# The end of the last batch of a two-layer attention kernel: partial products around the last sums, a separate sum buffer for GpSimd, later sums of the third pair

## The reference, cut to what matters

```python
xn = _group_norm(xf, gamma, beta)
qkv = jnp.einsum('oc,bcl->bol', w_qkv, xn) + b_qkv[None, :, None]
...
weight = jnp.einsum('bct,bcs->bts', q * scale, k * scale)
weight = jax.nn.softmax(weight.astype(jnp.float32), axis=-1).astype(q.dtype)
a = jnp.einsum('bts,bcs->bct', weight, v)
hid = a.reshape(b, c, L)
hid = jnp.einsum('oc,bcl->bol', w_proj, hid) + b_proj[None, :, None]
return (xf + hid).reshape(b, c, h, w)
```

## Time and profile before

| | us |
|---|---|
| median of 3 runs (lowest, highest) | 2491.03 (2490.61, 2492.5) |
| the profiled execution, own time | 2492.64 |
| its span in the trace | 2491.1 |
| TensorE busy, share of the span | 2438.5, 98% |
| VectorE, ScalarE, GpSimd busy | 1615.9, 1150.5, 1182.5 |
| stretch of pair 3 of the last batch, from its transpose of the maxima to its last weigh | 2413.9 to 2452.5 |
| stretch from there to the end of the span | 2452.5 to 2491.1 |

### The profile page before, as it was taken

One profiled execution on the slowest core, in us unless ns is written; L12 is line 12 of the kernel. 1 busy time (PEld: TensorE's weight loads), 2 busy tenths in 40 slices (PEclk: granted clock), 3 DMA queues, 4 the chain that ended last, 5 costly groups with the idle time before them and its releaser, 6 DMA issues. The chain is left out here.

```text
span 2491.1 us, 37555 instructions
## 1 busy us (share of the span) xinstructions
PE 2438.5 (98%) x12980; PEld 1615.9 (65%) x12980; DVE 1615.9 (65%) x2161; ACT 1150.5 (46%) x1499; POOL 1182.5 (47%) x590
## 2 busy tenths in 40 slices
PE   8999999999799999999999999999999999999988
PEld 7888888788655566557556655755665575557544
DVE  6455555455667766775777577567857756775776
ACT  3332233223355645654555456355555645553553
POOL 3330000000047665773766667377656755771762
PEclk8999999999899999999999999999999999999999
DMA  6431111013221242215122321512231241213002
GB/s 199 139 111 45 56 67 66 27 42 128 83 95 35 111 144 88 109 32 211 34 97 104 130 101 53 194 43 102 93 144 34 110 175 63 97 31 119 26 26 76
DMA packets 73401, 226.75 MB, mean 91 GB/s; under 512 B 12224, under 2 KB 12224, under 8 KB 72384
## 3 DMA queue, kind: packets, MB, share of 16 engines
q1 hardware_dynamic: 58720, 172.01, 19.6%
q0 software_dynamic: 14560, 52.96, 5.8%
HBM read 141.05 MB, written 71.30 MB: 85 GB/s over the span
## 5 line engine op out<-in xcount | busy, mean ns | idle before, releaser
L591 POOL TENSOR_TENSOR a_all<-a_all 128x1024 f32<-128x1024 f32 x410 | 1010.1, 2464 | 508.2 <-ACT a_all L816 473.3
L816 ACT ACTIVATE a_all<-psum 128x1024 f32<-128x1024 f32 x512 | 496.5, 1022 | 80.3 <-PE psum L1539 67.7
L1104 DVE TENSOR_REDUCE small<-psum 128x2 f32<-128x1024 f32 x326 | 399.6, 1226 | 172.3 <-PE psum L1509 172.1
L1558 PE MATMUL psum<-a_all 128*64 128x512 f32 x2048 | 495.7, 605 | 0.0
L1311 PE MATMUL psum<-r_all 128*128 128x512 f32 x1920 | 454.5, 395 | 6.9 <-DVE r_all L1198 5.8
L1311 PEld LDWEIGHTS psum<-r_all 128*128 128x128 f32 x1920 | 359.4, 189 | 101.6 <-DVE r_all L957 10.2
L1539 PE MATMUL psum<-r_all 64*128 64x512 f32 x3200 | 417.8, 393 | 2.0 <-ACT a_all L816 2.0
L1498 PE MATMUL psum<-r_all 128*128 128x512 f32 x1536 | 364.4, 396 | 5.6 <-DVE r_all L1217 5.6
L1539 PEld LDWEIGHTS psum<-r_all 64*128 64x128 f32 x3200 | 301.7, 186 | 73.2 <-ACT a_all L816 14.0
L1498 PEld LDWEIGHTS psum<-r_all 128*128 128x128 f32 x1536 | 286.0, 189 | 85.9 <-issue 24.4
L1558 PEld LDWEIGHTS psum<-a_all 128*64 128x64 f32 x2048 | 124.0, 136 | 232.5 <-issue 173.4
(11 more groups left out here) (147 smaller groups left out, 2450.9 us busy)
## 6 DMA issues: line engine op xcount, KB each, us to landing
r_all<-w_dram SPq DMA_DIRECT2D x48, 1024.0 KB, 4.9
xn_dram<-a_all POOLq DMA_DIRECT2D x56, 512.0 KB, 7.0
r_all<-xn_dram SPq DMA_DIRECT2D x7, 4096.0 KB, 15.3
a_all<-y_dram SPq DMA_DIRECT2D x9, 2048.0 KB, 10.8
a_all<-x SPq DMA_DIRECT2D x16, 1024.0 KB, 6.5
y_dram<-a_all SPq DMA_DIRECT2D x16, 1024.0 KB, 4.2
out<-a_all SPq DMA_DIRECT2D x32, 512.0 KB, 4.0
a_all<-sums SPq DMA_DIRECT2D x192, 64.0 KB, 2.0
```

Source lines behind the costliest of these rows:

```text
L591: pool.tensor_tensor(p_sum[:, :, cols], probs[:, 0, :, cols] if i == 1 else p_sum[:, :, cols], probs[:, i % SLOTS, :, cols], ALU.add).then ...
L816: act.activation(probs[:, i % SLOTS, :, cols], psum[half][:, :, :], ACT.Exp, scale=SCALE).then_inc(probs_ready, 1)
L1104: dve.reduce_max(max2[:, :, tile, half], psum[3][:, :, :], AX_X).then_inc(work_free, 2)
L1558: last = pe.matmul(psum[2][h * D:(h + 1) * D, half], v_t[:, i, head], probs[:, i % SLOTS, h, half * HALF:(half + 1) * HALF], start=(i == 0 ...
```

## The change

All of it is in the last batch (`last`), most of it in pair 3 (`not more`) and after.

- `sums` of pair 2 moves from the head of pair 3 to behind the scores of i = 2, and goes into psum[3] in place of psum[2]. Its copy on ScalarE stands behind the exponentials of i = 2, its reciprocals on VectorE behind the first and the second `add_last`.
- `end_add` of pair 2 moves from before `max_rows` to behind the two normalises of pair 1. The split of pair 1 on ScalarE moves from before the scores of pair 3 to behind the exponentials of i = 0. Normalise of pair 2 moves from behind `add_last(3)` to behind `add_last(5)`, its high parts to behind the exponentials of i = 7, its low parts to behind the last add.
- GpSimd's adds of pair 3 go into a buffer of their own (`end_sum`, over `y_row`), and no longer wait for the sums of pair 2. `add_last(1)` still does.
- The residual is loaded to `res_end` (over `xn`) during pair 2, and ScalarE scales it from there into `res32` after the last adds, ahead of the high parts of pair 3.
- The projection of half 0 is made in parts, in four banks: j = 0 and 1 of the first tile, then the last sums, j = 0 and 1 of the three others, j = 2 of all four, j = 3 of all four. Half 1 goes tile by tile, the wait for pair 3's split standing ahead of j = 3 of its first tile.
- The output is stored tile by tile, in eight stores of 256 KB.

The diff, cut:

```diff
+        res_end = f(xn[:, 0])
...
+        end_sum = y_row.rearrange("p (h n) -> p h n", h=2)
...
+        def end_bank(t):
+
+            i = t % 6
+            return (psum[3], psum[0], psum[2])[i // 2][:, i % 2]
...
-                if not last:
+                if last:
+
+                    sp.dma_start(res_end, y_v[b]).then_inc(res_loaded, 16)
+                else:
...
-                    sp.wait_ge(pv_done, ONE + (b + 1) * PAIRS * NT)
-                    sp.wait_ge(sum_step, LAST_SUMS + NT - 1)
-                    sp.wait_ge(last_sums, NT - 1)
+
+                    for t, (o, half) in enumerate(proj_tiles(last)):
+                        cols = slice(half * HALF, (half + 1) * HALF)
+                        sp.wait_ge(work_free, proj_used(b, t + 1, last))
+                        sp.dma_start(out_v[b, :, o, cols], res32[:, o, cols]).then_inc(out_stored[o // 2], 16)
...
-                sp.dma_start(res32, y_v[b]).then_inc(res_loaded, 16)
-                for o in range(CT):
-                    sp.wait_ge(work_free, proj_used(b, proj_tiles(last).index((o, NH - 1)) + 1, last))
-                    sp.dma_start(out_v[b, :, o], res32[:, o]).then_inc(out_stored[o // 2], 16)
...
+                    sp.dma_start(res32, y_v[b]).then_inc(res_loaded, 16)
+                    for o in range(CT):
+                        sp.wait_ge(work_free, proj_used(b, proj_tiles(last).index((o, NH - 1)) + 1, last))
+                        sp.dma_start(out_v[b, :, o], res32[:, o]).then_inc(out_stored[o // 2], 16)
...
-                sp.wait_ge(half, ONE + B * CT // 2 * 16)
+                sp.wait_ge(half, ONE + (B + 1) * CT // 2 * 16)
...
-                            if i == 1 and half == 0:
+                            if i == 1 and half == 0 and not last_pair:
...
-                            pool.tensor_tensor(p_sum[:, :, cols], probs[:, 0, :, cols] if i == 1 else p_sum[:, :, cols],
+                            to = end_sum if last_pair else p_sum[:, :, cols]
+                            pool.tensor_tensor(to, probs[:, 0, :, cols] if i == 1 else to,
                                                probs[:, i % SLOTS, :, cols], ALU.add).then_inc(sum_step, 1)
...
+            def scale_res(b, o, res):
+                if o == 0:
+                    act.wait_ge(res_loaded, (b + 1) * 16)
+                act.activation(res32[:, o], res[:, o], ACT.Identity, scale=bn_scale[:, o:o + 1],
+                               bias=res_bias[:, o:o + 1]).then_inc(res_scaled, 1)
...
-                        if p and not more and i == 2:
-                            copy_sums(b, p - 1)
-                        if p >= 2 and i == 2:
+                        if p >= 2 and more and i == 2:
                             for h in range(NH):
...
                         if p and more and i == 0:
-                            copy_sums(b, p - 1)
-                        if p and not more and i in (4, 5):
-                            hid_hi(b, p - 1, i - 4)
+                            copy_sums(b, p - 1, psum[2][:, 0])
+                        if not more:
+                            if i == 0:
+                                for h in range(NH):
+                                    hid_hi(b, p - 2, h)
+                            if i == 2:
+                                copy_sums(b, p - 1, psum[3][:, 0])
+                            if i == NT - 1:
+                                for h in range(NH):
+                                    hid_hi(b, p - 1, h)
...
-                    copy_sums(b, PAIRS - 1)
+                if last:
+
+                    act.wait_ge(sum_step, LAST_SUMS + NT - 1)
+                    act.wait_ge(last_sums, NT - 1)
+                    for o in range(CT):
+                        scale_res(b, o, res_end)
+                else:
+                    copy_sums(b, PAIRS - 1, psum[1][:, :, :])
...
-                act.wait_ge(res_loaded, (b + 1) * 16)
-                for o in range(CT):
-                    act.activation(res32[:, o], res32[:, o], ACT.Identity, scale=bn_scale[:, o:o + 1],
-                                   bias=res_bias[:, o:o + 1]).then_inc(res_scaled, 1)
+                if not last:
+                    for o in range(CT):
+                        scale_res(b, o, res32)
...
+                    if not more:
+                        end_add(pairs - 1)
...
-                        end_add(pairs)
+                        if p < PAIRS - 2 or not last:
+                            end_add(pairs)
                     else:
-                        invert_sums(b, p - 1, 0, CT)
                         for i in range(1, NT):
                             add_last(i, pairs)
-                            if i == CT - 1:
+                            if i in (1, 2):
+                                invert_sums(b, p - 1, (i - 1) * 2, 2)
+                            if i == 5:
                                 for h in range(NH):
                                     normalise(b, p - 1, h)
-                            if i in (5, 6):
-                                hid_lo(b, p - 1, i - 5)
+                        for h in range(NH):
+                            hid_lo(b, p - 1, h)
...
+                    if last:
+                        ps = end_bank(t)
...
-                        pe.wait_ge(sums_copied, ONE + pairs)
+                            pe.wait_ge(sums_copied, ONE + pairs)
...
-                    done = pe.matmul(to, ones64[:, 0:D if wide else QUARTER], p_sum[:, h, half * HALF:(half + 1) * HALF],
-                                     start=True, stop=True)
+                    of = end_sum[:, h] if last and half == 0 else p_sum[:, h, half * HALF:(half + 1) * HALF]
+                    done = pe.matmul(to, ones64[:, 0:D if wide else QUARTER], of, start=True, stop=True)
...
-                    if p and not more:
-
-                        pe.wait_ge(o_ready, ONE + pairs)
-                        sums(pairs - 1, psum[2][:, 0])
...
+                        if not more and i == 2:
+                            sums(pairs - 1, psum[3][:, 0])
                         next_max()
                         if i:
                             weigh(b, p, i - 1, more)
...
+                def proj_steps(to, o, half, js):
+                    cols = slice(half * HALF, (half + 1) * HALF)
+                    slot, piece = o // 2, o % 2
+                    for j in js:
+                        for k, (w, m) in enumerate(THREE):
+                            done = pe.matmul(to, w_s[:, slot, piece, w, j], hid[:, m, j, cols], start=(j == 0 and k == 0),
+                                             stop=(j == CT - 1 and k == 2))
+                    return done
+
+                def hid_made(pairs, half):
+                    pe.wait_ge(hid_lo_done, HID0 + (b * PAIRS + pairs) * NH - (NH - 1 - half))
...
+                tiles = proj_tiles(last)
                 if last:
-                    sums(b * PAIRS + PAIRS - 1, last=True)
+                    for slot in range(2):
+                        pe.wait_ge(ws_loaded[slot], (loads + 3) * 16)
+
+                    pe.wait_ge(sums_copied, ONE + b * PAIRS + PAIRS - 1)
+                    pe.wait_ge(probs_ready, ONE + (b + 1) * PAIRS * 2 * NT)
+                    hid_made(PAIRS - 2, NH - 1)
+                    for t in range(CT):
+                        work.next()
+                        proj_steps(end_bank(t), *tiles[t], range(CT - 2))
+                        if t == 0:
+                            sums(b * PAIRS + PAIRS - 1, last=True)
+                    hid_made(PAIRS - 1, NH - 1)
+                    for t in range(CT):
+                        proj_steps(end_bank(t), *tiles[t], (CT - 2,))
+                    hid_made(PAIRS, 0)
+                    for t in range(CT):
+                        proj_steps(end_bank(t), *tiles[t], (CT - 1,)).then_inc(work_full, 1)
+                    for t in range(CT, 2 * CT):
+                        n, _ = work.next()
+                        if t == CT:
+
+                            pe.wait_ge(o_ready, ONE + (b + 1) * PAIRS)
+                        if t >= 6:
+
+                            pe.wait_ge(work_free, n - 6)
+                        proj_steps(end_bank(t), *tiles[t], range(CT - 1))
+                        if t == CT:
+                            hid_made(PAIRS, 1)
+                        proj_steps(end_bank(t), *tiles[t], (CT - 1,)).then_inc(work_full, 1)
...
-                for t, (o, half) in enumerate(proj_tiles(last)):
-                    cols = slice(half * HALF, (half + 1) * HALF)
-                    slot, piece = o // 2, o % 2
-                    if o == 0:
-
-                        pe.wait_ge(hid_lo_done, HID0 + (b + 1) * PAIRS * NH - (NH - 1 - half))
-                    if half == 0 and piece == 0:
-                        n_load = (loads + 3 + slot) - (1 if last and slot else 0)
-                        pe.wait_ge(ws_loaded[slot], n_load * 16)
```

(35 more changed lines are left out.)

## The result

| | before | after |
|---|---|---|
| median (lowest, highest), us | 2491.77 (2490.61, 2492.75) | 2474.84 (2473.4, 2477.71) |
| ratio to before, 95% interval | | 0.9933 [0.9918, 0.9948] |
| profiled execution: own time, span | 2492.64, 2491.1 | 2477.71, 2476.1 |
| transpose of pair 3's maxima, last batch, start | 2413.94 | 2416.43 |
| from there to the end of the span (the *stretch*) | 77.2 | 59.7 |

The changed kernel is faster by 16.9 us in the medians. The two profiled executions differ by 15.0 only, because the one of after came 2.5 us later to the transpose. Ahead of it only one thing was changed, the residual's load, which SyncE issues at 2384.25. It doesn't explain the 2.5 us: the changed kernel's second profile, with the same load, reached the transpose at 2413.20.

What follows compares the result with a forecast made beforehand. TensorE was taken as the bound, 98% of the span, with two waits in the last batch. Head -5.95, last add +0.6, end -9.7, store -0.4 make -15.4 us: median 2491.03 becomes 2475.6, range 2472 to 2481.

Steps and rivals of the forecast that it cites:

- likeliest case: Whole kernel: all terms come out as summed, median 2475.6 us; chance 0.68.
- The head: Start of pair 3: scores no longer wait for pair 2's last add and sums; -5.95 us.
- the moved sums: Pair 2's sums, now behind the scores of i = 2, take 1.87 us of TensorE with nothing beside them.
- The last add: End of pair 3: VectorE's last add ends 2.85 us behind the last weigh, before 2.23; +0.6 us.
- the order of turns between VectorE and GpSimd: Pair 3's adds alternate; pair 2's two normalises run behind GpSimd's seventh add, which ends at 2445.9 us.
- The exclusion: VectorE's adds, normalises and low parts exclude GpSimd's adds; without any lock the sum would be 1.6 us shorter.
- The end: Last sums to last matmul: partial projection matmuls cover the wait, 20.4 us in place of 30.1; -9.7 us.
- The clock's part: At the end, the low clock over the first projection matmuls costs 2.5 us, part of the 9.7.
- Half 1's split: At the end, split ready at 2462.8 us, TensorE asks for it at 2463.05.
- The residual's move: Residual's load leaves the end, issued at about 2381.8 us, 70 us before use: worth nothing.
- the store: Last output store is half as large; gain between 0 and 0.8 us, taken as 0.4.
- The rival that the clock falls in a hole that is left: TensorE's remaining idle at head or last sums lowers the clock: 2476.7, 2478.1, or 2479.2 us with both; chance 0.13.

Runs made afterwards that it cites:

- old_head: Changed kernel with pair 3's head as before: `end_add`, sums, copy and high parts back ahead of the scores; ratio to kernel before 0.9961, stretch 66.2 us.
- end_add_first: Changed kernel with only pair 2's last add back before the spreading of the maxima; ratio to kernel before 0.9961, stretch 65.8 us.
- one_buffer: Changed kernel with GpSimd's adds of pair 3 in `p_sum` again, first add waiting for pair 2's sums; ratio to kernel before 0.9941, stretch 63.5 us.
- no_parts: Changed kernel with half 0's projection tile by tile behind the last sums, as before; ratio to kernel before 0.9967, stretch 69.3 us.
- no_parts_warm: no_parts plus 24 matmuls of no use in TensorE's wait behind the last sums; ratio to kernel before 0.9957, stretch 67.0 us.
- head_warm: end_add_first plus 20 matmuls of no use in the wait behind pair 3's transpose; ratio to kernel before 0.9948, stretch 63.9 us.
- before_warm: Kernel before plus 24 matmuls of no use in each of two waits, behind pair 3's transpose and the last sums; ratio 0.9996, stretch 75.9 us.

## Why the prediction was right, step by step

The forecast was the likeliest case, 2475.6; measured 2474.84. Its sum was 2.1 us too small, -15.4 in place of the stretch's -17.5. That the median came within 0.8 us is luck: the forecast starts from a median of 2491.03, which is 2491.77 in the table above (0.7), and the medians differ by 0.6 less than the stretches. Times below count from the transpose's start.

| step | forecast | measured |
|---|---|---|
| scores of i = 0 start | 1.7 | 1.74 |
| scores of i = 3 start (before: 19.5) | 13.6 | 12.53 |
| last weigh ends | 32.7 | 31.6 |
| last add ends behind it (before: 2.23) | 2.85 | 1.77 |
| sums' end to the last matmul's end (before: 30.1) | 20.4 | 20.6 |
| last output add's end to the end (before: 3.43) | 3.0 | 2.85 |

**The head, right in its mechanism, 1.0 short.** `old_head` and `end_add_first` show that the order in VectorE's queue held TensorE. The mis-sized term is the moved sums: "1.87 us", taken from 2420.47 to 2422.34, where the clock was at 1.2 GHz. At 2.4 GHz the same eight matmuls take 0.99, which is 0.88 of the 1.03 us. The row was right and its state wrong: I had read in rows 8 that the clock was low there, and did not apply it to this price. The trace of the kernel before has the price at the full clock too, for the same eight matmuls in pair 2 (timeline; 0.99 us from the sums' start to the next matmul):

```profile
2382.95 1.07 PE L1576 MATMUL psum<-a_all,small 128*32 128x512 f32 x8
...
2383.94 0.50 PE L1509 MATMUL psum<-u,r_all 64*128 64x512 f32 x2
```

**The last add, forecast 1.1 too late.** The second mis-sized term is the order of turns between VectorE and GpSimd, and by the rows it follows from the first. The sums were done 0.9 us earlier than drawn, so `add_last(1)` was issued at 2427.23, 0.18 us ahead of GpSimd's second add, and took 1.23 us; I had put it behind. VectorE kept its lead: its fourth and fifth add waited 0.26 and 0.39 us for exponentials. So the two normalises of pair 2 (1.15 us) ran in front of GpSimd's seventh add, where the forecast has them behind it, and only two adds stood between that add and the last sums. Rows of the changed kernel, GpSimd's second and seventh add and the two normalises:

```profile
2427.41 3.29 POOL L604 TENSOR_TENSOR a_all<-a_all 128x1024 f32<-128x1024 f32 x1
...
2441.70 3.46 DVE L1202 TENSOR_TENSOR a_all<-a_all 128x512 f32<-128x512 f32 x2
...
2444.91 2.49 POOL L604 TENSOR_TENSOR a_all<-a_all 128x1024 f32<-128x1024 f32 x1 [0.89 <-ACT a_all L833]
```

That the first term alone turned this order is read from the rows and was not tried apart. The exclusion itself holds: GpSimd's second add, issued inside VectorE's, ended 2.24 us behind it, and VectorE's sixth, issued at 2445.09, ended 1.07 us behind GpSimd's seventh (2447.40). In `one_buffer` a later start of GpSimd's adds came back as 2.2 us at the last add, with an upper bound of 2.4 expected. By the Trainium skill (SBUF — State Buffer, "Who interferes with whom") the order of issue decides which of the two is blocked. The trace agrees, in both of these pairs of rows; the order of issue is what I could not know to a microsecond.

**The end, right.** `no_parts` costs 9.6 against a forecast of 9.7. The clock's part of it is 2.3 (`no_parts_warm`), forecast 2.5. In the changed kernel itself this part came to 9.45 us, 0.25 short, since the 90 matmuls behind the sums take 0.230 each and not 0.227. Half 1's split was ready 0.2 us ahead of need by the forecast and no wait showed. The residual's move costs and brings nothing, as said; the store brings 0.6, forecast 0.4. For a store of 256 KB the Trainium skill (DMA: Bandwidth & Descriptors, "Anatomy of one DMA") would have an estimated 2.6 us to landing, but its formula is for transfers that GpSimd issues, and the prediction applied it to SyncE's without saying so. The trace has 2.2; the formula's difference between the two sizes, 0.6, is the measured one.

**Clock and cover apart.** By `head_warm` and `no_parts_warm` 1.9 us of the head and 2.3 of the end are the clock; together 4.2 of 17.5. The rest is work in places where TensorE had none. Undone one at a time, head, parts and stores make 6.5 + 9.6 + 0.6 = 16.7. The 3.8 of `one_buffer` don't belong in this sum: in the kernel before the sums stood ahead of pair 3's adds, and GpSimd's first of them waited for ScalarE and not for the sums. So by the rows the own buffer only keeps the moved sums from costing something. The 0.8 left was not tried apart; the later place of pair 2's normalises, for one, was never undone. The rival that the clock falls in a hole that is left did not come to pass: the clock stayed at 1.00 in both profiles of the changed kernel. But it was near. In `one_buffer` and `before_warm` the clock fell within 0.4 us of the last sums' start, and they took 1.5 and 1.4 us longer.

## What to carry to other kernels

When one engine is full but for a few waits, look at which instruction stands ahead in the queue of the engine that ends them: one add of 1.2 us, issued before a spreading that TensorE waited for, cost 6.1 us here, 1.9 of them by the clock, because the add itself waited for a third engine. A product over several sources can be started with those sources that are ready, one open bank for each tile; this hides as much work as the wait is long, if the banks are there. Price a moved instruction from a row at the clock it will run at, and give a wait like those of 2.20 to 2.52 us here the price of a fall of the clock behind it: three of the four that were read had one.

## What the runs showed of the hardware

- A wait of TensorE of 2.38 us before the last sums was followed by a fall of the clock in `before_warm`, and a wait of the same 2.38 us at the same place of the kernel before by none until 2460.5. A wait of 2.20 us and one of 2.52 (`one_buffer`) were each followed by a fall; one of 1.90 at this place (`no_parts`) was not. So the length of the wait alone does not decide it; what does was not tried.
- The eight matmuls of `sums` take 0.99 us when each makes 32 rows (pair 2's sums) and 1.87 when each makes 64 (the last sums), both at 2.4 GHz and 512 columns.
- With nothing ahead of it changed but the residual's load, the start of the stretch lay between 2412.5 and 2417.1 us in the profiled executions. A profile taken once can't show a change of under 5 us here in its span, but it can in a stretch.
